# Turning the token blocks of a routed feed-forward by VectorE and a DRAM trip instead of by TensorE

## What is computed

```python
logits = jnp.einsum('btd,de->bte', x, gate_w)
expert_weights, expert_indices = jax.lax.top_k(softmax(logits), 2)   # then divided by their sum
for i in range(E):
    wi = jnp.where(expert_indices == i, expert_weights, 0.0).sum(-1)
    h = silu(x @ w1[i]) * (x @ w3[i])
    out = out + (h @ w2[i]) * wi[..., None]
```

## Time and profile before

| what | value |
|---|---|
| median of three runs | 444.62 us (444.39 to 445.95) |
| the profiled execution | 445.63 us, its span 443.8 us |
| TensorE matmuls busy | 405.7 us, 91% of the span |
| VectorE / ScalarE / POOL busy | 303.2 / 193.7 / 243.2 us |
| DMA traffic | 89.82 MB, mean 202 GB/s |
| granted TensorE clock, mean | 0.97 of full speed |

### The profile page before, as it was taken

The page is one execution under the profiler, slowest core; times in us unless marked ns, Lnnn a source line. Parts: engine busy times, 40 slices in busy tenths (PEclk is TensorE's granted clock), DMA queues, the critical chain, the costliest instruction groups (busy, mean ns, idle before and its releaser), DMA issues.

```text
span 443.8 us, 12041 instructions
## 1 busy us (share of the span) xinstructions
PE 405.7 (91%) x2300; PEld 338.6 (76%) x2305; DVE 303.2 (68%) x826; ACT 193.7 (44%) x335; POOL 243.2 (55%) x251
## 2 busy tenths in 40 slices
PE   0669899969899999999999999999999999999983
PEld 0557686536678888888888888888888888788873
DVE  7995959887775577647775775577587546857450
ACT  2573527104543454335544553455445335634341
POOL 6328444313664676546665685576577445435443
PEclk9997969698999999999999999999999999999998
DMA  6953996702895788567887787789788655465652
GB/s 188 356 172 100 303 358 206 289 26 58 265 278 177 198 259 246 178 168 194 243 264 209 228 250 205 194 247 251 202 265 254 197 159 152 127 154 130 166 144 36
DMA packets 80362, 89.82 MB, mean 202 GB/s; under 512 B 8071, under 2 KB 60583, under 8 KB 80343
## 3 DMA queue, kind: packets, MB, share of 16 engines
q1 hardware_dynamic: 64327, 55.24, 38.4%
q0 software_dynamic: 16016, 34.37, 30.7%
HBM read 58.77 MB, written 30.82 MB: 202 GB/s over the span
## 4 chain that ended last, share of the span: by engine, by line
PE 70%; issue 3%; DVE 3%; ACT 1%; DMA 1%; DVEq 1%; POOL 0%; ACTq 0%; POOLq 0%
PE bank L1545 67%; PE bank L1552 2%; ACT split L341 1%; DMA out<-yblk,itok 1%; PE bank L1488 1%; DVE onehot_lo L1173 0%; POOL out L546 0%; ACT yblk L718 0%; DVE hT L1288 0%; DVE hmul L1272 0%; DVEq L295 0%; DVE swap_in L1280 0%; ACTq L341 0%; PE bank L1481 0%; DVE ctx_sb L951 0%
## 5 line engine op out<-in xcount | busy, mean ns | idle before, releaser
L1545 PE MATMUL bank<-split,xT_hi 128*128 x592 | 166.1, 402 | 4.4 <-issue 2.7
L1545 PEld LDWEIGHTS bank<-split,xT_hi 128*128 128x128 f32 x592 | 106.5, 189 | 27.9 <-issue 8.6
L1545 PEld LDWEIGHTS bank<-split,hT 128*128 128x128 f32 x888 | 111.5, 189 | 5.5 <-issue 1.5
L1545 PE MATMUL bank<-split,hT 128*128 (+1 forms) x888 | 113.3, 284 | 1.4 <-ACT yblk L718 0.7
L711 ACT ACTIVATE gact<-bank 128x512 f32<-128x512 f32 x74 | 44.3, 598 | 138.5 <-PE bank L1545 136.2
L1272 DVE TENSOR_TENSOR hmul<-gact,bank 128x512 f32<-128x512 f32 x74 | 50.8, 686 | 74.4 <-ACT gact L711 73.8
L1545 PE MATMUL bank<-split,xT_lo 128*128 x296 | 92.2, 393 | 0.0
L529 POOL DMA_INDIRECT xblk<-z_rows,gidx x40 | 41.0, 1024 | 89.6 <-DVE gidx L1295 69.8
L546 POOL DMA_INDIRECT out<-yblk,itok x37 | 71.0, 1919 | 32.1 <-issue 29.6
L347 DVE TENSOR_TENSOR split<-raw,split x22 | 50.3, 2292 | 25.9 <-ACT split L341 24.2
L1545 PEld LDWEIGHTS bank<-split,xT_lo 128*128 128x128 f32 x296 | 55.6, 188 | 12.3
(11 more groups left out here) (199 smaller groups left out, 336.0 us busy)
## 6 DMA issues: line engine op xcount, KB each, us to landing
raw<-in_L_ffn_w POOLq DMA_DIRECT2D x84, 256.0 KB
swap_rows<-swap_in SPq DMA_DIRECT2D x74, 256.0 KB, 3.7
swap_out<-swap_rows SPq DMA_DIRECT2D x74, 256.0 KB, 3.7
ctx_sb<-in_ctx SPq DMA_DIRECT2D x4, 1024.0 KB, 6.4
raw<-in_L_ffn_w SPq DMA_DIRECT2D x12, 256.0 KB, 6.6
x_all<-in_x SPq DMA_DIRECT2D x4, 512.0 KB, 8.4
depool_rows<-gact SPq DMA_DIRECT2D x4, 512.0 KB, 4.0
out<-x_all SPq DMA_DIRECT2D x4, 512.0 KB, 6.2
```

Of the source, the lines that this page charges most:

```text
L1545: mm = pe.matmul(out_, xp, w_, start=start and n == 0, stop=stop and n == 2)
```

## The change

For the blocks from 2 on the transposes leave TensorE. At the head of step i VectorE copies the indices of block i+3 and transposes the 32x32 squares of block i+2 (`tokens_turned`) as soon as its gather has landed. SP sends the 128 KB to a new DRAM buffer (`tokens_out`) ahead of the first swap, and fetches it back (`tokens_in`) with the squares in their places, between the first and the second swap out, after a wait for the way out. The way back is 512 runs of 256 bytes. One step later, where ScalarE and VectorE made xT_hi and xT_lo from PSUM, they make them from the fetched tile (`xT_turned`). POOL's step waits for the turn of block i+1, which is done a step earlier, in place of TensorE's transposes. The tiles of the trip lie over tiles of the first stage (win, ginit, bin). Blocks 0 and 1 go the old way.

```diff
--- before.py
+++ after.py
@@ -76,6 +76,7 @@
 
         z_dram = nc.dram_tensor("z_rows", (T + P, D), f32, kind="Internal").ap()
         w_dram = nc.dram_tensor("w_rows", (2 * T, 1), f32, kind="Internal").ap()
+        turn_dram = nc.dram_tensor("turn_rows", (2, P, D), f32, kind="Internal").ap()
         swap_dram = nc.dram_tensor("swap_rows", (2, 2, P, HALF), f32, kind="Internal").ap()
         depool_dram = [nc.dram_tensor(f"depool_rows{b}", (S, D), f32, kind="Internal").ap() for b in range(B)]
 
@@ -92,8 +93,9 @@
         win = sb("win", [P, KD, D], f32)
         gres = sb("gres", [P, KD], f32)
         gate = sb("gate", [P, KD, E], f32)
-        ginit = sb("ginit", [P, D], f32)
-        bin_ = sb("bin", [P, D], f32)
+        gains = sb("gains", [P, 2, D], f32)
+        ginit, bin_ = gains[:, 0], gains[:, 1]
+        turn_in, turn_out = (t[:, :, :].rearrange("p q (b k t) -> p q b k t", b=NQ, k=KD) for t in (win, gains))
         zeros = sb("zeros", [P, D], f32)
 
 
@@ -253,7 +255,7 @@
             blocks_ready bf16_ready idx_ready z_rows tbl_step table_ready
             raw_first raw_ready hi_ready lo_first lo_ready x1_rows added_rows
             up0_done up1_done silu0_done silu1_done h0_done h1_done
-            swap_ready hT0hi_ready hT0lo_ready hT1hi_ready hT1lo_ready xT_done xThi_ready xTlo_ready
+            swap_ready hT0hi_ready hT0lo_ready hT1hi_ready hT1lo_ready xT_done turn_ready xThi_ready xTlo_ready
             gidx_ready widx_ready meta_ready y_done y_ready settled_pool settled_sp""".split()
         s = {n: sem(n) for n in names}
         x_in = [sem(f"x_in{b}") for b in range(B)]
@@ -264,6 +266,8 @@
         blk_in = [sem(f"blk_in{q}") for q in range(2)]
         wtok_in = [sem(f"wtok_in{q}") for q in range(2)]
         parked = [[sem(f"parked{q}_{part}") for part in range(2)] for q in range(2)]
+        turn_parked = [sem(f"turn_parked{q}") for q in range(2)]
+        turned_in = [sem(f"turned_in{q}") for q in range(2)]
         swapped = [[sem(f"swapped{q}_{part}") for part in range(2)] for q in range(2)]
 
         block = stack.enter_context(nc.Block(no_gpsimd_drain=True))
@@ -427,8 +431,28 @@
 
             sp.wait_ge(s["table_ready"], 1)
 
+            def tokens_out(i, q, half):
+
+                sp.wait_ge(s["turn_ready"], i + 1)
+                if after(i, 2):
+                    settle(sp)
+                    sp.wait_ge(turned_in[q], 16 * half)
+                    settle(sp)
+                sp.dma_start(turn_dram[q], turn_in[:, q].rearrange("p b k t -> p (b k t)")).then_inc(turn_parked[q], 16)
+
+            def tokens_in(i, q, half):
+
+                sp.wait_ge(turn_parked[q], 16 * (half + 1))
+                if after(i, 2):
+                    settle(sp)
+                    sp.wait_ge(s["xTlo_ready"], i + 1)
+                    settle(sp)
+                sp.dma_start(turn_out[:, q].rearrange("p a k t -> p a (k t)"),
+                             turn_dram[q].rearrange("(a j) (b c) -> (j b) a c", a=NQ, b=NQ)).then_inc(turned_in[q], 16)
+
             def exchange(i, q, half):
 
+                tokens_out(i, q, half)
                 for part in range(2):
                     sp.wait_ge(s["swap_ready"], 2 * i + part + 1)
                     if after(i, 2):
@@ -437,6 +461,8 @@
                         settle(sp)
                     sp.dma_start(swap_dram[q, part], swap_in[:, q, part].rearrange("p b k t -> p (b k t)"))\
                       .then_inc(parked[q][part], 16)
+                    if part == 0:
+                        tokens_in(i, q, half)
                 for part in range(2):
                     sp.wait_ge(parked[q][part], 16 * (half + 1))
                     if after(i, 2):
@@ -452,6 +478,8 @@
             less_two = blocks_less_two(sp)
             over_steps(sp, step)
             for q in range(2):
+                sp.wait_ge(turned_in[q], ((less_two + 3 - q) >> 1) * 16)
+                settle(sp)
                 for part in range(2):
                     sp.wait_ge(swapped[q][part], ((less_two + 3 - q) >> 1) * 16)
                     settle(sp)
@@ -575,7 +603,10 @@
             def step(i, q, half, word):
 
                 e = expert(word)
-                pool.wait_ge(s["xT_done"], i + 2)
+                if after(i, 1):
+                    pool.wait_ge(s["turn_ready"], i)
+                else:
+                    pool.wait_ge(s["xT_done"], 2)
                 settle(pool)
                 load_piece(e, word, 0)
                 block_rows(i + 3, 1 - q)
@@ -706,6 +737,12 @@
                 act.activation(hT_hi[:, q, ks].rearrange("p k (a t) -> p a k t", a=NQ), swap_out[:, q, part], ACT.Copy)\
                    .then_inc(s[f"hT{part}hi_ready"], 1)
 
+            def xT_turned(q, count):
+
+                act.wait_ge(turned_in[q], 16 * count)
+                act.activation(xT_hi[:, q].rearrange("p k (a t) -> p a k t", a=NQ), turn_out[:, q], ACT.Copy)\
+                   .then_inc(s["xThi_ready"], 1)
+
             def silu(i, half):
                 act.wait_ge(s[f"up{half}_done"], i + 1)
                 act.activation(gact[:, half * HALF:(half + 1) * HALF], p_gate[half][:, :], ACT.Silu)\
@@ -719,7 +756,10 @@
 
             def step(i, q, half, word):
                 silu(i, 0)
-                xT(i + 1, 1 - q)
+                if after(i, 1):
+                    xT_turned(1 - q, half + q)
+                else:
+                    xT(i + 1, 1 - q)
                 if after(i, 2):
                     hT(q, half, 1)
                 silu(i, 1)
@@ -1289,6 +1329,20 @@
                                   hT_hi[:, q, ks].bitcast(f32).rearrange("p k (a t) -> p a k t", a=NQ), ALU.subtract)\
                    .then_inc(s[f"hT{part}lo_ready"], 1)
 
+            def tokens_turned(i, q, half):
+
+                dve.wait_ge(blk_in[q], 16 * (half + 2))
+                if after(i, 2):
+                    dve.wait_ge(turn_parked[q], 16 * half)
+                dve.transpose(turn_in[:, q].rearrange("p b k t -> p k b t"),
+                              xblk[:, q, :].rearrange("p (k t b) -> p k b t", b=NQ, t=Q)).then_inc(s["turn_ready"], 1)
+
+            def xT_turned(i, q):
+                dve.wait_ge(s["xThi_ready"], i + 1)
+                dve.tensor_tensor(xT_lo[:, q].rearrange("p k (a t) -> p a k t", a=NQ), turn_out[:, q],
+                                  xT_hi[:, q].bitcast(f32).rearrange("p k (a t) -> p a k t", a=NQ), ALU.subtract)\
+                   .then_inc(s["xTlo_ready"], 1)
+
             def next_index(i, q, half):
 
                 dve.wait_ge(blk_in[q], 16 * half)
@@ -1317,12 +1371,16 @@
                 if not after(i, 1):
                     dve.wait_ge(s["lo_first"], 2)
                     dve.sem_inc(s["lo_ready"], 2)
+                next_index(i + 3, 1 - q, half + q + 1)
+                tokens_turned(i, q, half)
                 h(i, 0)
                 turn(i, q, half, 0)
-                xT(i + 1, 1 - q)
+                if after(i, 1):
+                    xT_turned(i + 1, 1 - q)
+                else:
+                    xT(i + 1, 1 - q)
                 if after(i, 2):
                     hT(i - 2, q, 1)
-                next_index(i + 3, 1 - q, half + q + 1)
                 weight_index(i, q, half)
                 h(i, 1)
                 turn(i, q, half, 1)
@@ -1583,7 +1641,8 @@
                     pe.wait_ge(s["lo_first"], 1)
 
                 up(slot, q, 0)
-                xT(i + 1, 1 - q, half + q)
+                if not after(i, 1):
+                    xT(i + 1, 1 - q, half + q)
 
                 if after(i, 1):
                     pe.wait_ge(s["h1_done"], i)
```

## The result

Before took 444.5 us in the comparison, after **464.32 us** (462.46 to 467.94, four runs): slower, ratio 1.046 with a 95% interval of 1.038 to 1.055.

A forecast was written before the change was run, and what follows sets the result against it. TensorE's matmuls and transposes were taken to bound the kernel from step 4 on. Transposes -7.9, VectorE +0.8, start +5.5 and SP's queue +8.5 summed to +6.9 us: 451.5 as a median, range 438.5 to 468.

The forecast's parts named there:

- SP's two landings in line: SP's queue: waits for the block's way out and the second swap out stand one behind the other in each step.
- the likeliest case: Whole kernel: slower, 451.5 us as a median, own range 446 to 459, chance 0.50.
- Transposes, -7.9: TensorE, steps after step 0: 36 pairs of transposes go at 0.22 us each, 7.9 us gained.
- VectorE, +0.8, and its turn at 0.41: VectorE: the 128x256 turn takes 0.41 us, covered by idle time except once, after the step with two splits: 0.8 lost.
- The start, +5.5: First steps: VectorE waits for block 2's gather, then early trips land late; step 4 at 140.3 instead of 135.46, 5.5 us lost.
- SP's queue, +8.5: SP in loaded steps: two landings in series make blocks late, 1.7 us per phase, five phases, 8.5 us lost.
- The rival "much slower", 467.5: Trip's way back: 256-byte runs cost as much as 512-byte ones, both landings 5.3, phases cost 24.5 us; chance 0.17.
- The rival "faster": SP's queue: both landings fit in a step because half the bytes land in half the time; 439.4 us, chance 0.21.
- What would show it: Profile signs: 8.49 us unloaded steps, ScalarE and SP waits, gaps before mid down product, step 2 after 118, step 4 near 140.

The follow-up runs named there:

- e1: Changed kernel with SP fetching the block back after the second swap out instead of between the two swaps out: 453.77 us, ratio 1.023.
- e2: Changed kernel with the weight loads issued in the loop fetching only an eighth of their bytes: 445.73 us, ratio 1.003.
- e5: Changed kernel with the block fetched after the second swap out and the copies to xT_hi and xT_lo behind the second silu and second h: 444.67 us, ratio 1.002.
- e3: Kernel before the change, with the trip's transfers added on SP's queue, of unused data and without a same-step wait: 445.38 us, ratio 1.004.
- e10: Changed kernel with VectorE's turn reading its source in order instead of every fourth element: 458.65 us, one run.
- e6: e5 with block 2 also going the old way by TensorE, and step 0's turn and trip behind everything else of their step: 442.93 us, ratio 0.999.

## Why the prediction was right or wrong

**Direction and mechanism: right, the size too small.** The forecast was slower by SP's two landings in line. e1, e2 and e5 show that this is the cause: with SP's order mended half of the loss goes, with light loads nearly all of it in the middle, with both orders mended most of it; and e3 shows that the same transfers cost little when nobody waits for them in the same step. The forecast of 451.5 was 12.8 too low; 464.32 lies in the range, but above the 446 to 459 of the likeliest case alone. Term by term:

- *Transposes, -7.9.* As TensorE's busy time they are worth a little more than priced: 7.9 for the 32 pairs of steps 4 to 36, where 36 pairs were to bring that. As time of the kernel they are worth less. From the earlier trace rows a pair of steps takes 17.41; in after an undisturbed pair takes 8.48 + 8.69 = 17.17. Won are 0.24 a pair and not 0.44, about 4 us over 36 steps. The step that failed: "a microsecond taken from TensorE within a step is a microsecond of the kernel". For steps that jump it is not (D), though the earlier trace rows already showed that these take 0.25 longer than the others, which the prediction read and did not ask about. The 390 ns that the prediction quotes from the Trainium skill stand there for a bf16 transpose, and these are f32; the row decided, so the sum does not hang on it.
- *VectorE, +0.8, and its turn at 0.41.* The turn took 0.63, inside the bounds, for the stride (e10). In the head of a step it was covered by idle time, as assumed: VectorE waited 1.6 us in the whole run for a gather ahead of it. The step in which it was not to be covered, step 32, took 10.62 us, before 10.59: with the 0.22 that it does not win this is 0.25, where 0.8 was taken.
- *The start, +5.5.* Steps 0 to 4 grew by 4.8. Counted from step 0, step 1 was forecast 8.4 later and came at 8.3 (108.69), step 2 was forecast at 16.3 and came at 15.5 (115.89), step 3 at 28.3 and came at 28.4, step 4 at 38.0 and came at 37.9. Step 2 was 0.8 early and then 0.9 longer than forecast, with a gap of 2.8 us in its down product and slow matmuls behind it, so that the later steps fit so well is partly luck. And block 2's trip weighed less than its share in the working: e6 no longer waited for it and kept 36.4.
- *SP's queue, +8.5.* The term that was mis-sized. With what it won less from the transposes, the middle lost 19.4 + 3.8 = 23.2. On average the landings are not the reason. The chain shows the long ones (5.39, 4.60 and 5.43 above), but over the 15 loaded steps the block's way out took 4.3 us on average (4.2 was taken) and the second swap out 3.9 (4.8 was taken); the way back, in the 13 of these steps in which ScalarE waited for it, took 3.6 (5.3 was taken). What was too small is SP's own time between the last issue of a step and the next block's: 1.45 to 3.09 us in these steps, 2.06 on average, where the working has one issue of 0.4. It is no shorter without a load (at least 1.45, and 1.99 where the loop jumps), so there SP starts the next block 3.3 to 4.0 us into a step (steps 33 to 36) and not at 2.4. With the measured averages put in, the prediction's own working gives about 3 us a phase, 15 in all (an estimate). What is left has no term in the working: the clock behind the gaps, 4.2 us, the waits at the heads of steps behind a late hT, and the scatter of the landings (block out 2.4 to 6.4, second swap out 2.4 to 5.6), of which only the late ones count. How the rest divides between these is not shown.
- *The rival "much slower", 467.5.* By price the nearest, with 24.5 for the middle, but not for its reason: it put both landings at 5.3, and they took 4.3 and 3.9 on average. Runs of 256 bytes were not slower than runs of 512 either: the way back took 2.2 to 5.5 us in loaded steps, where a swap in took 5.3 before. No run tests the size of the runs by itself. That the price came out near is chance.
- *The rival "faster"* asked for the block's out and the second swap out together under some 8 us in loaded steps; they took 5.6 to 10.3, on average 8.2. So it was near the line. Its premise is not seen: without a load the block's way out took 1.9 to 3.4 us to SP's next issue, the second swap out, with twice the bytes, 2.1 to 2.8.
- *What would show it.* ScalarE's copy waiting for the way back (38.4 us in all), SP's waits on the block out and on swaps, and gaps ahead of the middle of the down product came as written. 8.49 us for a step without a load came in every second step only (8.48 and 8.69). Step 4 near 140 came (138.29); step 2 after 118 did not (115.89), since step 0 began 1.9 earlier and step 2 was early.

## What to carry to other kernels

A new round trip on a queue that already waits for its own transfers costs landings in series, in the steps where the memory is busy, and nothing in the others: price it with the loaded landing, add the queue's own instructions from one step's last issue to the next step's first (here five times the single issue that was counted), and look who stands behind the waiting engine. Take a gap in TensorE as more than its length, since the clock comes back later than the work and the next step's head can wait for the same late tile once more. And where two kinds of step differ in length though they do the same matmuls, find out why before counting what fewer matmuls will bring: here that question alone, with no trip at all, was worth 1%.

## What had not been expected of the hardware

- After 4.2 us without matmuls the granted clock was 0.50 to 0.53 for the next 5.2 us of matmuls; over steps 4 to 36 two such stretches, with 8.5 us of matmuls, made them an estimated 4.2 us dearer.
- The next step starts no sooner than 2.73 us behind the end of hT's second half in a step that jumps, and 2.34 in one that does not, before and after alike, also when the matmuls end earlier.
- From the last issue of a step to the first of the next, SP's queue took at least 1.45 us, and 1.99 where its loop jumps, with no landing to wait for.
- VectorE's transpose of 128x256 took 0.63 us with a source of stride 4, 0.44 without; that of 128x512 without a stride 0.71.
- Two transfers a step, 128 KB each and waited for by nobody in the same step, cost the old kernel 3.1 us in 32 steps (e3); with the waits in line the middle lost 23.2.
- From its issue to SP's next issue, 128 KB out took no less than 256 KB out: 4.3 and 3.9 us on average in loaded steps, 1.9 to 3.4 and 2.1 to 2.8 without a load.
